# A gated cross-attention and expert kernel: GpSimd's scaling work and Newton steps dealt over the steps by a table, and VectorE's y tiles in two-tensor form

## The chip, the cores and the metric

One core of one Trainium2 chip runs the whole kernel. The metric is the device time of one execution in microseconds. The kernel before has a median of 321.2 us over 3 runs (321.14 to 321.3).

## The reference

Two residual blocks over x of shape (2, 1024, 256), all in float32:

```
x = x + tanh(g_xattn) * xattn(layernorm(x), ctx)     # 16 heads of 64, 64 context tokens
x = x + tanh(g_ffn)  * ffn(layernorm(x))             # 8 experts, top 2 of a sequence
layernorm(x) = (x - mean) / sqrt(var + 1e-5)
xattn: q = x Wq, k = ctx Wk / 8, v = ctx Wv, softmax(q k^T) v Wo + bo
ffn:   router on the mean over a sequence of layernorm(x); softmax, top 2 of 8
       sum over the two experts of  weight * (gelu(h w1 + b1) w2 + b2),  F = 1024
```

## The kernel before, in words

The 2048 tokens are 16 tiles of 128 tokens, t = 0 to 15; the first eight belong to sequence 0. After a setup of some 20 us, in which Wq and Wk are folded into one matrix and Wv and Wo into another, the attention runs as a software pipeline written out by hand: `run_steps` calls `step(s)` for s = -2 to 18 on every engine, each engine with its own order of work, and semaphores that count tiles tie them together. The order in the code is the order on the engine.

Every product is taken in three matmuls of rounded parts (high with high, high with low, low with high), so most tiles exist as `_hi` (written by ScalarE) and `_lo` (the rest, written by VectorE).

What tile t goes through, and at which step:

- x_scaled(t), only t >= 6, GpSimd, step t-2: `xs`, the raw x that was loaded already transposed, has the mean taken off and is multiplied with the reciprocal deviation. Both statistics lie in `spread`, where a DMA has copied them to all partitions. Tiles 0 to 5 are normalised untransposed (`xn`) and transposed by TensorE.
- x_high and x_low, ScalarE and VectorE, step t-1: `xT_hi`, `xT_lo`.
- scores(t), TensorE, step t: 12 matmuls of 512 columns.
- max(t) (L903), then the subtraction for 8 heads (L910), VectorE, step t; heads(t), ScalarE, step t: the exponentials of the other 8 heads (L636), right after max(t). The exponential of the first half follows at step t+1 (L625).
- sum and reciprocal (L873, L878), VectorE, step t+1; mul(t), GpSimd, step t+1: the product with the reciprocal in two halves (L504).
- transposes of tile t (L1238), TensorE, step t+2, then pT_high(t) (L648, ScalarE), pT_low(t) (L862, VectorE), then the value product, TensorE, which ends step t+2.
- residual(t) (L949) and its statistics (L954), VectorE, step t+3.

At steps 5 and 7 TensorE, ScalarE and VectorE also make the last four groups of the value matrix ("value groups": L1211, L600, L813); heads(s) stands behind them on ScalarE.

The second layernorm starts inside this pipeline. For each four tiles VectorE makes mean, variance and a first guess of the reciprocal root in eight small instructions on 4 columns (`norm` part 0, L762 to L770, called as `y_guess`, at steps 6, 10 and 14); GpSimd refines the guess by three Newton steps (`y_rstds`, L470 to L476, 13 small instructions that each wait for the one before) at the head of steps 7, 11 and 15, ahead of mul; VectorE then makes y tiles 0 to 7 (`y_tile`, L969) at the ends of steps 7 to 12, TensorE transposes them (L1326), and ScalarE and VectorE split them (L975). The same `norm` serves x: `x_norm(2)` for tiles 8 to 15 at VectorE's step 4, and its Newton steps at the end of GpSimd's step 4, whose result goes by DMA into `spread`. On GpSimd the order within a step is: y_rstds, `xn`, mul(s-1), x_scaled(s+2), Newton steps for x.

Behind the attention come the two experts of each sequence, in 64 pieces, TensorE with little idle time.

Of the kernel before, what the change touches and what calls it, by code (L numbers as in the profile page):

```python
# [5 lines left out]
def gated_cross_attention_moe_kernel(nc, x, xT, ctx_tokens, g_xattn, g_ffn, Wq, Wk, Wv, Wo, bo,  # L6
# [5 lines left out]
    ALU = mybir.AluOpType  # L12
# [4 lines left out]
    P = 128  # L17
# [18 lines left out]
    EPS = 1e-5  # L36
# [30 lines left out]

    stats2 = stats1
    mean1 = place("mean1", [P, NT])
    rstd1 = place("rstd1", [P, NT])  # L70
    mean2 = place("mean2", [P, NT])
    rstd2 = place("rstd2", [P, NT])
# [103 lines left out]
    with stack:  # L176
        ps = stack.enter_context(nc.psum_tensor("ps", [P, 8, BANK], f32))

        def sem(name):
            return stack.enter_context(nc.semaphore(name))  # L180
# [27 lines left out]
        rep_ready, logits_done, idx_ready, gap_ready, gap_done, sel_ready = (  # L208
            sem(n) for n in ("rep_ready", "logits_done", "idx_ready", "gap_ready", "gap_done", "sel_ready"))
        stat_out, stat_in, xT_raw, xT_ready = (sem(n) for n in ("stat_out", "stat_in", "xT_raw", "xT_ready"))  # L210
        y_rstd, x_rstd, xn_by_dve, w1_first = sem("y_rstd"), sem("x_rstd"), sem("xn_by_dve"), sem("w1_first")
        staged_w1 = [sem("staged_w1_0"), sem("staged_w1_1")]
        staged_half = [sem("staged_half_0"), sem("staged_half_1")]
# [132 lines left out]
        X_PARTS = [(0, TB // 2), (TB // 2, TB), (TB, NT)]  # L346

        X_BY_DVE = X_PARTS[1][0]
        SPREAD_PARTS = [(XT0, TB), (TB, NT)]
        x_stat = [nc.dram_tensor(f"x_stat_{i}", (2, P, t1 - t0), f32, kind="Internal").ap()  # L350
                  for i, (t0, t1) in enumerate(SPREAD_PARTS)]
# [10 lines left out]
        def active(t):  # L362
            return 0 <= t < NT
# [81 lines left out]
        @block.gpsimd  # L445
        def _(pool):
            nc.gpsimd.memset(ident[:, :], 0.0).then_inc(zeros_ready, 1)
            pool.wait_ge(zeros_ready, 1)
            nc.gpsimd.affine_select(out=ident[:, :], in_=ident[:, :], compare_op=ALU.not_equal, fill=1.0,
                                    base=0, pattern=[[-1, P]], channel_multiplier=1).then_inc(ident_ready, 1)  # L450
            nc.gpsimd.memset(ones_row[:, :], 1.0).then_inc(rows_ready, 1)
            for e in range(E):
                last = nc.gpsimd.memset(iota[:, e:e + 1], float(e))
            last.then_inc(rows_ready, 1)

            pn = [0]

            def link(ins):

                pn[0] += 1  # L460
                ins.then_inc(pool_step, 1)
                pool.wait_ge(pool_step, pn[0])

            def newton(t0, t1, rstd, var, guess):

                r, n = rstd[:, t0:t1], t1 - t0
                v, u = ve_p[:, 0:n], nu_p[:, 0:n]
                tt, ts = nc.gpsimd.tensor_tensor, nc.gpsimd.tensor_scalar
                pool.wait_ge(guess_ready, guess)
                link(ts(v, var[:, t0:t1], -0.5, None, ALU.mult))  # L470
                for _ in range(3):

                    link(tt(u, v, r, ALU.mult))
                    link(tt(u, u, r, ALU.mult))
                    link(ts(u, u, 1.5, None, ALU.add))
                    link(tt(r, u, r, ALU.mult))  # L476

            def y_rstds(i):

                newton(*Y_PARTS[i], rstd2, ve_y, len(X_PARTS) + i + 1)  # L480
                pool.sem_inc(y_rstd, 1)

            def step(s, par):
                if s in (7, 11, 15):
                    y_rstds((s - 7) // 4)
                t = s + LEAD
                if active(t) and t < XT0 and t != X_BY_DVE:

                    wait_pos(pool, xT_done, t - 1)
                    tile = xt[:, ds(t, 1), :].rearrange("p o d -> p (o d)")  # L490
                    nc.gpsimd.tensor_tensor(xn[:, par, :], tile, mean1[:, ds(t, 1)].broadcast_to([P, D]),
                                            ALU.subtract).then_inc(xc_ready, 1)
                    pool.wait_ge(xc_ready, t + (t < X_BY_DVE))
                    nc.gpsimd.tensor_tensor(xn[:, par, :], xn[:, par, :], rstd1[:, ds(t, 1)].broadcast_to([P, D]),
                                            ALU.mult).then_inc(xn_ready, 1)
                t = s - 1
                if active(t):
                    q = (par - 1) % 2

                    pool.wait_ge(recip_done, t + 1)  # L500
                    for half in range(2):
                        hs = slice(half * H // 2, (half + 1) * H // 2)
                        pr = sx[:, q, half * BANK:(half + 1) * BANK].rearrange("p (h m) -> p h m", m=M)
                        nc.gpsimd.tensor_tensor(pr, pr, rs[:, q, hs].unsqueeze(2).broadcast_to([P, H // 2, M]),  # L504
                                                ALU.mult).then_inc(mul_done, 1)
                if active(s + LEAD) and s + LEAD >= XT0:
                    x_scaled(s + LEAD)
                if s == 1:
                    newton(*X_PARTS[1], rstd1, ve_x, 2)
                    pool.sem_inc(x_rstd, 1)  # L510
                if s == 4:
                    newton(*X_PARTS[2], rstd1, ve_x, 3)
                    pool.sem_inc(x_rstd, 1)

            def x_scaled(t):

                i = next(i for i, (t0, t1) in enumerate(SPREAD_PARTS) if t < t1)
                mean, rstd = (spread[i][:, row, :, t - SPREAD_PARTS[i][0]].unsqueeze(1).broadcast_to([P, KD, P])
                              for row in range(2))
                pool.wait_ge(xT_raw, 32)  # L520
                pool.wait_ge(stat_in, 16 * (i + 1))
                nc.gpsimd.tensor_tensor(x_raw(t), x_raw(t), mean, ALU.subtract).then_inc(xc_ready, 1)  # L522
                pool.wait_ge(xc_ready, t)
                nc.gpsimd.tensor_tensor(x_raw(t), x_raw(t), rstd, ALU.mult).then_inc(xT_ready, 1)  # L524

            pool.wait_ge(guess_ready, 1)
            run_steps(step)


            pool.wait_ge(sel_ready, 1)  # L530
            for t in range(TB, NT):
                if t == Y_PARTS[3][0]:
                    pool.wait_ge(guess_ready, len(X_PARTS) + 4)
                pool.wait_ge(yT_done, t - 1)
                nc.gpsimd.tensor_tensor(yb[:, t % 2, :], xt[:, t, :], mean2[:, t:t + 1].broadcast_to([P, D]),
                                        ALU.subtract).then_inc(xc_ready, 1)
                pool.wait_ge(xc_ready, NT + t - TB)
                nc.gpsimd.tensor_tensor(yb[:, t % 2, :], yb[:, t % 2, :], rstd2[:, t:t + 1].broadcast_to([P, D]),
                                        ALU.mult).then_inc(y_ready, 1)
# [204 lines left out]
        def _(dve):  # L744
# [8 lines left out]
            def norm(t0, t1, mean, rstd, var, parts=range(4)):  # L753


                tiles, n = slice(t0, t1), t1 - t0
                me, ce, mo, co = (stats1[:, tiles, i] for i in (1, 2, 4, 5))
                m, r = mean[:, tiles], rstd[:, tiles]
                v, d, u = var[:, tiles], dm[:, 0:n], nu[:, 0:n]
                tt, ts, stt = nc.vector.tensor_tensor, nc.vector.tensor_scalar, nc.vector.scalar_tensor_tensor  # L760
                if 0 in parts:
                    tt(d, me, mo, ALU.subtract)  # L762
                    tt(m, me, mo, ALU.add)
                    link(tt(v, ce, co, ALU.add))
                    ts(m, m, 0.5, None, ALU.mult)
                    tt(d, d, d, ALU.mult)
                    link(ts(v, v, 1.0 / D, EPS, ALU.mult, ALU.add))
                    link(stt(v, d, 0.25, v, ALU.mult, ALU.add))

                    link(ts(r.bitcast(i32), v.bitcast(i32), -0.5, float(0x5F3759DF), ALU.mult, ALU.add))  # L770
                for part in (1, 2, 3):
                    if part in parts:

                        link(stt(u, v, -0.5, r, ALU.mult, ALU.mult))
                        link(tt(u, u, r, ALU.mult))
                        link(stt(r, u, 1.5, r, ALU.add, ALU.mult))
# [53 lines left out]
                                        ALU.subtract).then_inc(xlo_ready, 1)  # L830

            nc.vector.memset(warm_w[:, :], 0.0).then_inc(warm_ready, 1)
            dve.sem_inc(hlo_ready, FREE_GELS)
            group("ctxT", 0)
            x_stats(0, range(0, 2))
# [129 lines left out]
            def y_tile(t):  # L965

                dve.wait_ge(y_rstd, t // 4 + 1)
                wait_pos(dve, yT_done, t - 1)
                nc.vector.tensor_scalar(yb[:, t % 2, :], xt[:, t, :], mean2[:, t:t + 1], rstd2[:, t:t + 1],  # L969
                                        ALU.subtract, ALU.mult).then_inc(y_ready, 1)  # L970

            def y_low(t, bank, c0, until):

# [550 lines left out]
```

## Time and profile before

| | before |
|---|---|
| median of 3 runs | 321.2 us (321.14 to 321.3) |
| the profiled execution | 321.67 us, its span 319.7 us |
| granted TensorE clock | 0.999 of full speed |
| TensorE matmul busy | 313.2 us, 98% |
| VectorE busy | 236.5 us, 74% |
| ScalarE busy | 164.6 us, 52% |
| GpSimd busy | 84.5 us, 26% |

The profile is one execution with a start and a duration for every instruction. A row of a timeline gives the start in us from the span's start, the duration in us, the engine, the line, the operation and its tiles; "x2" means two merged instructions, and a bracket tells how long the engine had been idle and what released it. PE is TensorE, DVE is VectorE, ACT is ScalarE, POOL is GpSimd. Durations of neighbours can overlap a little, so the distance between two starts is the better measure of what an instruction costs its engine. The attention pipeline fills the time from about 23 to 140 us.

### The profile page before, as it was taken

Reading aid. Unit: us, or ns where it says so; the run is one execution under the profiler, and the core shown is the slowest. Engines: PE = TensorE matmul, PEld = TensorE weight load, DVE = VectorE, ACT = ScalarE, POOL = GpSimd, SP = SyncE. Lnnn points to the kernel's source line nnn. Section 1 sums busy time; section 2 is a strip of 40 time slices with the busy share of each in tenths; the row PEclk is TensorE's granted clock in tenths of the full one; section 3 lists DMA queues with packets and bytes.
Section 4 is the critical chain, followed back from the end, with each engine's and each line's share of the span. In section 5 each row is a group of like instructions: output and inputs, shape, how many; then the busy total and the mean of one; then the engine's idle time right before and its main releaser. Section 6 shows DMA issues by size and latency. Waiting matters only on the chain.

```text
span 319.7 us, 5709 instructions
## 1 busy us (share of the span) xinstructions
PE 313.2 (98%) x1861; PEld 269.9 (84%) x1861; DVE 236.5 (74%) x563; ACT 164.6 (52%) x577; POOL 84.5 (26%) x158
## 2 busy tenths in 40 slices
PE   8999999999999999999999999999999999999996
PEld 7878998878988999888788888888887899888896
DVE  1889999989989999999998475466767554442643
ACT  2648565686766768766366254444543442321320
POOL 1325547586476655425600000000000000000000
PEclk9999999999999999999999999999999999999999
DMA  7997300300000009500016250000020000000012
GB/s 261 386 330 9 35 3 1 133 1 3 0 0 3 0 2 331 195 3 0 2 8 255 79 187 0 0 0 0 24 99 11 2 0 0 2 0 0 2 66 67
DMA packets 21918, 19.99 MB, mean 63 GB/s; under 512 B 11708, under 2 KB 17540, under 8 KB 21508
## 3 DMA queue, kind: packets, MB, share of 16 engines
q1 hardware_dynamic: 21616, 19.14, 19.9%
q10 hardware_dynamic: 276, 0.52, 0.4%
q8 instruction: 14, 0.23, 0.3%
q14 instruction: 12, 0.10, 0.1%
HBM read 17.56 MB, written 2.11 MB: 62 GB/s over the span
## 4 chain that ended last, share of the span: by engine, by line
PE 71%; POOL 10%; DVE 7%; issue 7%; DMA 2%; ACT 2%; SPq 0%; POOLq 0%; DVEq 0%
PE ps L1153 22%; PE ps L1154 22%; PE ps L1155 22%; POOL sx L504 4%; DMA xt<-in_x_dram 2%; POOL xs L524 2%; PE ps L1238 2%; POOL xs L522 2%; ACT sx L636 1%; DVE mx L903 1%; PE ps L1173 1%; DVE pT_lo L862 1%; PE ps L1326 1%; DVE sm L873 1%; PE ps L1424 1%
## 5 line engine op out<-in xcount | busy, mean ns | idle before, releaser
L723 ACT ACTIVATE gel<-ps,b1sel 128x512 f32<-128x512 f32 x64 | 43.9, 690 | 95.5 <-PE ps L1155 95.4
L1112 DVE CAST h_hi<-gel 128x512 fp32r<-128x512 f32 x64 | 28.4, 444 | 58.8 <-ACT gel L723 58.5
L636 ACT ACTIVATE sx<-ps,mx 128x64 f32<-128x64 f32 x128 | 38.3, 325 | 26.2 <-DVE mx L903 26.1
L1153 PE MATMUL ps<-yT_hi,w_hi 128*128 128x512 f32 (+1 forms) x128 | 50.5, 395 | 0.0
L1154 PE MATMUL ps<-yT_lo,w_hi 128*128 128x512 f32 (+1 forms) x128 | 50.0, 390 | 0.0
L1155 PE MATMUL ps<-yT_hi,w_lo 128*128 128x512 f32 (+1 forms) x128 | 49.9, 390 | 0.0
L1114 DVE TENSOR_TENSOR h_lo<-gel,h_hi 128x512 fp32r<-128x512 f32 x64 | 44.9, 702 | 2.2
L504 POOL TENSOR_TENSOR sx<-sx,rs 128x512 f32<-128x512 f32 x32 | 33.5, 1066 | 41.5 <-DVE rs L878 40.8
L1153 PE MATMUL ps<-h_hi,w_hi 128*128 128x512 f32 x96 | 38.4, 400 | 0.0
L1155 PE MATMUL ps<-h_hi,w_lo 128*128 128x512 f32 x96 | 37.5, 390 | 0.0
L1154 PE MATMUL ps<-h_lo,w_hi 128*128 128x512 f32 x96 | 37.4, 390 | 0.0
L1153 PE MATMUL ps<-vw,pT_hi 128*128 128x256 f32 x128 | 36.6, 286 | 0.1
L1155 PE MATMUL ps<-vw,pT_lo 128*128 128x256 f32 x128 | 36.2, 283 | 0.0
L1154 PE MATMUL ps<-vw,pT_hi 128*128 128x256 f32 x128 | 36.2, 283 | 0.0
L1155 PEld LDWEIGHTS ps<-yT_hi,w_lo 128*128 128x128 f32 x128 | 24.0, 188 | 5.1
L1153 PEld LDWEIGHTS ps<-yT_hi,w_hi 128*128 128x128 f32 x128 | 24.1, 188 | 4.6
L1154 PEld LDWEIGHTS ps<-yT_lo,w_hi 128*128 128x128 f32 x128 | 24.1, 188 | 4.4
L636 ACT ACTIVATION_READ_ACCUMULATOR sx<-ps,mx 128x1 f32 x128 | 27.8, 217 | 0.0
L1153 PE MATMUL ps<-a_hi,xT_hi 128*128 128x512 f32 x64 | 26.5, 413 | 0.1
L1153 PEld LDWEIGHTS ps<-vw,pT_hi 128*128 128x128 f32 x128 | 24.4, 191 | 2.0 <-issue 1.4
L1155 PE MATMUL ps<-a_hi,xT_lo 128*128 128x512 f32 x64 | 25.1, 392 | 0.0
L1154 PE MATMUL ps<-a_lo,xT_hi 128*128 128x512 f32 x64 | 25.0, 390 | 0.0
(149 smaller groups left out, 670.3 us busy)
## 6 DMA issues: line engine op xcount, KB each, us to landing
stage_w<-in_L_ffn_w_dram SPq DMA_DIRECT2D x7, 1024.0 KB, 7.4
out_dram<-xt SPq DMA_DIRECT2D x6, 256.0 KB, 2.3
wqT<-in_L_xattn_Wq_dram SPq DMA_DIRECT2D x2, 512.0 KB, 7.2
wv_sb<-in_L_xattn_Wv_dram SPq DMA_DIRECT2D x2, 512.0 KB, 8.8
wo_sb<-in_L_xattn_Wo_dram SPq DMA_DIRECT2D x1, 1024.0 KB, 13.9
xt<-in_x_dram SPq DMA_DIRECT2D x1, 1024.0 KB, 10.6
xs<-in_xT_dram SPq DMA_DIRECT2D x1, 1024.0 KB, 11.1
spread<-x_stat SPq DMA_DIRECT2D x1, 1024.0 KB, 4.6
```

What stands on the lines that cost most here:

```text
L504: nc.gpsimd.tensor_tensor(pr, pr, rs[:, q, hs].unsqueeze(2).broadcast_to([P, H // 2, M]), ALU.mult).then_inc(mul_done, 1)
L522: nc.gpsimd.tensor_tensor(x_raw(t), x_raw(t), mean, ALU.subtract).then_inc(xc_ready, 1)
L524: nc.gpsimd.tensor_tensor(x_raw(t), x_raw(t), rstd, ALU.mult).then_inc(xT_ready, 1)
L636: last = nc.scalar.activation(sx[:, par, c0:c0 + M], ps[:, 2 * par + 1, c0 - BANK:c0 - BANK + M], ACT.Exp, bias=mx[:, par, h:h + 1], accum ...
L723: nc.scalar.activation(gel[:, f % 4, :], ps[:, h_bank, :], ACT.Gelu, bias=b1sel[:, b, slot, f:f + 1]).then_inc(gelu_done, 1)
L862: nc.vector.tensor_tensor(pT_lo[:, par, 4 * half:4 * half + 4, :], ps[:, 4 + half, :].rearrange("p (m i) -> p m i", m=4), as_f32(pT_hi[:, ...
L1112: nc.vector.tensor_copy(h_hi[:, f % 4, :], gel[:, f % 4, :]).then_inc(hhi_ready, 1)
L1114: nc.vector.tensor_tensor(h_lo[:, f % 4, :], gel[:, f % 4, :], as_f32(h_hi[:, f % 4, :]), ALU.subtract).then_inc(hlo_ready, 1)
L1153: mm(acc, hi_w, hi_x, start=start, stop=False)
L1154: mm(acc, hi_w, lo_x, start=False, stop=False)
L1155: return mm(acc, lo_w, hi_x, start=False, stop=stop)
L1238: last = nc.tensor.transpose(ps[:, 4 + half, m * P:(m + 1) * P], sx[:, par, c0:c0 + P], ident[:, :])
```

## The change

Four things. (1) x_scaled follows a table: tiles 6 and 7 at step 3 (before: 4 and 5), tile 12 at step 9 beside tile 11 (before: 10); the others stay. (2) GpSimd's Newton steps for y: the first at the head of step 6 (before: 7), the second in step 10 behind mul(9) (before: head of 11), the third stays at 15. (3) `norm` part 0 has seven instructions for eight, none of them but the guess in the one-tensor form: the mean is d * -0.5 + the first half's mean, and EPS comes from a column in SBUF, broadcast. It has five waits on itself for four. (4) `y_tile` is a scalar_tensor_tensor with the reciprocal deviation as a broadcast tensor, for a tensor_scalar with two per-partition scalars.

```diff
+    eps_col = place("eps_col", [P, 1])
+        SCALE_AT = {3: (6, 7), 6: (8,), 7: (9,), 8: (10,), 9: (11, 12), 11: (13,), 12: (14,), 13: (15,)}
@@ gpsimd
             def step(s, par):
-                if s in (7, 11, 15):
-                    y_rstds((s - 7) // 4)
+                if s in (6, 15):
+                    y_rstds((6, 10, 15).index(s))
...
-                if active(s + LEAD) and s + LEAD >= XT0:
-                    x_scaled(s + LEAD)
+                if s == 10:
+                    y_rstds((6, 10, 15).index(s))
+                for t in SCALE_AT.get(s, ()):
+                    x_scaled(t)
@@ vector, norm
                     tt(d, me, mo, ALU.subtract)
-                    tt(m, me, mo, ALU.add)
                     link(tt(v, ce, co, ALU.add))
-                    ts(m, m, 0.5, None, ALU.mult)
-                    tt(d, d, d, ALU.mult)
-                    link(ts(v, v, 1.0 / D, EPS, ALU.mult, ALU.add))
+                    stt(m, d, -0.5, me, ALU.mult, ALU.add)
+                    link(stt(v, v, 1.0 / D, eps_col[:, 0:1].broadcast_to([P, n]), ALU.mult, ALU.add))
+                    link(tt(d, d, d, ALU.mult))
                     link(stt(v, d, 0.25, v, ALU.mult, ALU.add))
@@ vector, at the start
+            nc.vector.memset(eps_col[:, :], EPS).then_inc(eps_ready, 1)
+            dve.wait_ge(eps_ready, 1)
@@ vector, y_tile
-                nc.vector.tensor_scalar(yb[:, t % 2, :], xt[:, t, :], mean2[:, t:t + 1], rstd2[:, t:t + 1],
-                                        ALU.subtract, ALU.mult).then_inc(y_ready, 1)
+                nc.vector.scalar_tensor_tensor(yb[:, t % 2, :], xt[:, t, :], mean2[:, t:t + 1],
+                                               rstd2[:, t:t + 1].broadcast_to([P, D]), ALU.subtract,
+                                               ALU.mult).then_inc(y_ready, 1)
```

## Rows read from the trace of the kernel before

**Rows 1.** The page, part 1: busy us (share of the span) xinstructions.
```profile
PE 313.2 (98%) x1861; PEld 269.9 (84%) x1861; DVE 236.5 (74%) x563; ACT 164.6 (52%) x577; POOL 84.5 (26%) x158
```

**Rows 2.** The page, part 4: the chain that ended last, by engine.
```profile
PE 71%; POOL 10%; DVE 7%; issue 7%; DMA 2%; ACT 2%; SPq 0%; POOLq 0%; DVEq 0%
```

**Rows 3.** Waits of PE: us in total, times, longest us.
```profile
PE ps L1238 <- POOL sx L504: 0.9, 3, 0.3
```

**Rows 4.** Timeline of DVE, steps 6 and 7: the loop.
```profile
61.35 1.21 DVE L903 TENSOR_REDUCE mx<-ps 128x16 f32<-128x1024 f32 x1
...
65.60 1.29 DVE L862 TENSOR_TENSOR pT_lo<-ps,pT_hi 128x512 fp32r<-128x512 f32 x2 [1.52 <-ACT pT_hi L648]
...
67.96 1.21 DVE L903 TENSOR_REDUCE mx<-ps 128x16 f32<-128x1024 f32 x1
```

**Rows 5.** Timeline of ACT, steps 5 to 7.
```profile
49.41 1.12 ACT L648 ACTIVATE pT_hi<-ps 128x512 fp32r<-128x512 f32 x2
...
64.92 1.13 ACT L648 ACTIVATE pT_hi<-ps 128x512 fp32r<-128x512 f32 x2
...
67.85 1.27 ACT L600 ACTIVATE vw<-ps,tg 128x512 fp32r<-128x512 f32 x2 [0.98 <-PE ps L1211]
```

**Rows 6.** Timeline of DVE, step 4's x_norm(2) and pT_low behind it.
```profile
47.77 0.72 DVE L763 TENSOR_TENSOR mean<-stats 128x8 f32<-128x8 f32 x1
...
48.61 0.70 DVE L765 TENSOR_SCALAR mean<-mean 128x8 f32<-128x8 f32 x1
...
50.83 1.27 DVE L862 TENSOR_TENSOR pT_lo<-ps,pT_hi 128x512 fp32r<-128x512 f32 x2
```

**Rows 7.** Timeline of POOL, steps 4 to 9: scaling, Newton steps, mul.
```profile
47.72 0.74 POOL L522 TENSOR_TENSOR xs<-xs,spread 128x256 f32<-128x256 f32 x1
...
50.02 0.24 POOL L470 TENSOR_SCALAR ve_p<-ve_x 128x8 f32<-128x8 f32 x1 [0.73 <-DVEq L794]
...
54.10 2.04 POOL L504 TENSOR_TENSOR sx<-sx,rs 128x512 f32<-128x512 f32 x2 [0.18 <-POOL rstd L476]
...
61.23 2.09 POOL L504 TENSOR_TENSOR sx<-sx,rs 128x512 f32<-128x512 f32 x2 [3.58 <-DVE rs L878]
63.29 0.85 POOL L522 TENSOR_TENSOR xs<-xs,spread 128x256 f32<-128x256 f32 x1
...
65.10 0.23 POOL L470 TENSOR_SCALAR ve_p<-ve_y 128x4 f32<-128x4 f32 x1
...
82.03 2.10 POOL L504 TENSOR_TENSOR sx<-sx,rs 128x512 f32<-128x512 f32 x2 [3.00 <-DVE rs L878]
```

**Rows 8.** Timeline of DVE, step 6's y_guess and pT_low behind it.
```profile
57.77 0.17 DVE L762 TENSOR_TENSOR dm<-stats 128x4 f32<-128x4 f32 x1
...
57.93 0.16 DVE L764 TENSOR_TENSOR ve_y<-stats 128x4 f32<-128x4 f32 x1
58.12 0.17 DVE L765 TENSOR_SCALAR mean<-mean 128x4 f32<-128x4 f32 x1
...
58.99 1.29 DVE L862 TENSOR_TENSOR pT_lo<-ps,pT_hi 128x512 fp32r<-128x512 f32 x2
```

**Rows 9.** Timeline of PE: the first matmul of scores(7), step 7.
```profile
63.80 0.48 PE L1153 MATMUL ps<-a_hi,xT_hi 128*128 128x512 f32 x1
```

**Rows 10.** Timeline of DVE, y_tile(0) and pT_low(6), steps 7 and 8.
```profile
71.13 1.02 DVE L969 TENSOR_SCALAR yb<-xt,mean,rstd 128x256 f32<-128x256 f32 x1
...
72.86 1.27 DVE L862 TENSOR_TENSOR pT_lo<-ps,pT_hi 128x512 fp32r<-128x512 f32 x2
```

**Rows 11.** Timeline of DVE, step 10's y_guess and pT_low behind it.
```profile
86.00 0.17 DVE L762 TENSOR_TENSOR dm<-stats 128x4 f32<-128x4 f32 x1
...
87.21 1.29 DVE L862 TENSOR_TENSOR pT_lo<-ps,pT_hi 128x512 fp32r<-128x512 f32 x2
```

**Rows 12.** Groups of DVE by form: busy us, mean ns of one, idle before.
```profile
L894 DVE TENSOR_TENSOR xT_lo<-xs,xT_hi 128x256 fp32r<-128x256 f32 x10 | 3.6, 361 | 0.0
...
L883 DVE TENSOR_SCALAR xn<-xt,mean,rstd 128x256 f32<-128x256 f32 x1 | 0.3, 327 | 0.0
```

More of the change, by code:

```diff
@@ L210, in gated_cross_attention_moe_kernel @@
         stat_out, stat_in, xT_raw, xT_ready = (sem(n) for n in ("stat_out", "stat_in", "xT_raw", "xT_ready"))
+        eps_ready = sem("eps_ready")
         y_rstd, x_rstd, xn_by_dve, w1_first = sem("y_rstd"), sem("x_rstd"), sem("xn_by_dve"), sem("w1_first")
```

## The prediction

> **What bounds the kernel now.** I read the page's busy line first: TensorE is busy for 98% of the span, so anything that helps must take away idle or late TensorE work, and the whole reserve is some 6 us of 319.7 [rows 1]. The chain of waits then gives GpSimd 10% of the chain's length, far more than its share of necessary work would suggest, and VectorE 7% [rows 2]. The waits of TensorE put only 0.9 us on GpSimd's mul [rows 3]. That is the first hint: direct stalls are small, and what counts is how a late instruction travels round the pipeline. So I went to the timelines of the four engines and followed one step.
>
> The timelines show a loop between VectorE and ScalarE. max(6) starts at 61.35, pT_high(5) at 64.92 once heads(6) is done, pT_low(5) at 65.60 (0.68 behind pT_high), and max(7) at 67.96: 6.61 us for a step [rows 4, 5]. From pT_low to the next max are 2.36; from the start of max to pT_high 3.57, of which max with its handover takes 1.24 and heads 2.33. Hence, whatever makes pT_low late makes every later tile late, unless TensorE is later still. pT_low can be late for two reasons: VectorE is not free yet, or heads on ScalarE started late. I work out both, place by place, as the lateness of this loop against before.
>
> How the engines disturb each other is in two rows. GpSimd's first scaling instruction of tile 6 runs from 47.72 to 48.46 [rows 7]. VectorE's L763, an addition of 8 columns with both inputs in SBUF, starts at 47.77 and takes 0.72, to 48.49, and L765 takes 0.70 the same way behind the second scaling instruction [rows 6]; without GpSimd beside them such instructions take 0.16 to 0.17 [rows 8]. L763 is a two-tensor instruction, L765 a one-tensor one: both forms are held to the end of GpSimd's instruction. A two-tensor form doesn't escape.
>
> **The change, part by part.**
>
> *x_scaled(6) and (7) at step 3.* They leave step 4 and take with them the two holds on x_norm(2): (0.72 - 0.16) + (0.70 - 0.17) = 1.1 us. The new form of x_norm costs 0.05 more (below). pT_low(3), which stands behind, can't start before pT_high(3) at 49.41 plus 0.68 = 50.09; it started at 50.83. The loop gains 0.74, the rest of the 1.1 is VectorE waiting. At step 3 the pair (1.6 us) fits into GpSimd's idle time before mul(3), since GpSimd idles 3.6 us before a mul [rows 7]. Value: -0.74; bounds 0 (should `spread` land late and the pair slip back) and -0.74.
>
> *Newton steps at the head of step 6.* They can start only when y_guess(0) ends, which in the new kernel is 58.99 - 0.74 + 0.05 = 58.3 [rows 8]. From the first Newton instruction to the mul behind it took 54.10 - 50.02 = 4.08; some of that was waiting for others, and I take 3.9. So mul(5) starts at 62.2. It started at 61.23 and, with the loop 0.74 ahead, could start at 60.5 [rows 7]. mul(5) is thus 1.7 late against what it could be, and 1.0 late against before. TensorE's second half of transposes needs it, and scores(7) moves from 63.80 to 64.8 [rows 9]. Behind scores(7) come the value groups of step 7; ScalarE's part of these waited for TensorE at 67.85 and takes 1.27 [rows 5]; it moves to 68.8 and ends at 70.0. heads(7) stands behind it, and before it started with the end of max(7), 67.96 + 1.24 = 69.2. So heads(7) is 0.8 late.
>
> *Newton steps gone from step 7.* They began at 65.10 and by the same 4.08 made mul(6) start at 69.2 [rows 7], though reciprocal(6) is done before max(7) at 67.96 [rows 4]. y_tile(0) then met the scaling of tile 9 head on, and was held for 1.02 us instead of 0.33 [rows 10, 12]; pT_low(6) started at 72.86, when ScalarE would have allowed 67.96 + 3.57 + 0.68 = 72.2. In the new order mul(6) starts at 67.2, scaling ends at 67.2 + 2.06 + 1.81 = 71.1, y_tile(0) comes at 70.9 and is held little. But ScalarE is late now: heads(7) at 70.0 + 2.33 + 0.68 gives pT_low(6) at 73.0. Against 72.86 that is +0.1. The 0.74 is used up: this place costs 0.84. Bounds: 0.1 (if mul(5) is only 0.3 late in effect) and 1.3 (all of 58.3 + 4.08 passed on, and the hold too).
>
> *x_scaled(12) at step 9, against y_guess(1) at step 10.* mul(8) starts at 82.03 + 0.1; it takes 2.06, each scaling pair 1.81 (63.29 to 65.10) [rows 7]. Tile 11 is at work from 84.2 to 86.0 and tile 12 from 86.0 to 87.8. y_guess(1) starts at 86.00 + 0.1 [rows 11]: exactly beside tile 12's two instructions, where GpSimd was idle before. By the rows of x_norm(2) its small instructions are held twice for most of a scaling instruction, and the chain gets on by one or two of its seven before GpSimd is through at 87.8; the remaining five take about 0.9. y_guess(1) ends at 88.7 instead of 87.21, and pT_low(8) directly behind it starts when it ends, before as after. Value: +1.4 on top of the +0.1; bounds 0.05 (no hold) and 1.8 (no progress in the gap).
>
> *Newton steps behind mul(9).* From 3.9 us in front of mul(10) they go into GpSimd's idle time behind mul(9), with x_scaled(12) cleared out of their way. This frees TensorE of a wait in step 12 (one of the three in rows 3), but the loop was ahead of mul(10) only on TensorE's side; I count nothing, bounds -0.4 and 0.
>
> *The small instructions of norm.* The starts are 0.08 apart without a wait between them and 0.19 with one (57.77, 57.93, 58.12) [rows 8]. Eight with four waits took 1.22 (57.77 to 58.99); seven with five take 0.05 more. Twice this stands in pT_low's way, but it is contained above.
> The Trainium skill (VectorE: DVE Perf Modes, Rules for kernel authors) says to minimise the number of operations, not the semaphores; by that seven for eight would save about 0.15, and the sum would be 0.3 us less. The rows bear it out only for instructions that wait anyway.
>
> *y_tile in two-tensor form.* The nearest rows are 0.36 for a two-tensor 128x256 in SBUF and 0.33 for the old form [rows 12]; a second per-partition operand less, a full stream more. Most tiles are held by a scaling instruction as before. I take 0.1 for each of eight and hide it in the 0.68 between pT_high and pT_low, except in steps 11 and 12 with two tiles each, where VectorE is already the later one; there VectorE later also waits for less (the routing step), so I count 0. Bounds -0.3 and +0.5. The new EPS column costs one small memset in the setup, where VectorE waits for loads: nothing.
>
> **The sum**, against the profiled execution of 321.67 us (span 319.7): -0.74 + 0.84 + 1.4 + 0 = +1.5, so 323.2 for a profiled execution. The median before is 0.47 lower, 321.2; hence 322.7. TensorE has so little idle time after the attention that nothing there takes up a later start.
>
> **Rivals.**
>
> *A: VectorE's small instructions slip past GpSimd.* If y_guess(1) is not held, the 1.4 goes: -0.74 + 0.84 + 0.05 = +0.15, 321.3. For it: L764, the instruction between the two held ones, wasn't held (L763 ends at 48.49 and L765 starts at 48.61 [rows 6]). Against it: the two that didn't, and that the chain needs every one of its instructions.
>
> *B, the other side: faster.* One mechanism: Newton in step 6 delays nobody. mul(5) is late, but pT_high(5) can't start before heads(6) ends at 64.2, and if the value groups of step 7 have slack, the place costs nothing and keeps the unheld y_tile(0) (-0.65) beside the -0.74. It decides if mul(5)'s second half is through by 63.3 as before, that is, if Newton's 13 instructions take under 3.0 us. With y_guess(1) half held (+0.7) that gives -0.7, 320.5; with it unheld -1.35, 319.9. Against it: the 4.08 us in the rows.
>
> *C: the late mul(5) also pushes x_scaled(8).* Its scaling would end at 62.2 + 2.06 + 1.81 = 66.1, and ScalarE wants it once pT_high(5) and the exponential are done, some 1.5 us behind the 64.3 at which pT_high(5) begins (an estimate from the 1.13 of rows 5). If this slips by 0.5, step 8 starts later: +0.7 more, 323.4 to 323.8.
>
> **Chances.** Forecast (322.0 to 323.3): 0.50; C: 0.10; A: 0.22; B: 0.18. A measurement of this kernel can tell 0.2% (0.64 us) from no change: slower 0.60 (forecast and C), the same 0.22 (A), faster 0.18 (B). The range of 320.4 to 323.8 takes in A and C and the upper part of B. The forecast's own range is 322.0 to 323.4.
>
> **What would show it.** Right: L763's successor in x_norm(2) at its plain 0.16 and pT_low(3) at about 50.1; mul(5) at about 62.2, directly behind L476; the value groups on ScalarE at 68.8; two instructions of y_guess(1) near 0.7 us each, and max(10) 1.5 us later than the 89.9 at which 87.21 + 2.36 + about 0.33 for y_low (an estimate from the 0.36 of rows 12) puts it. Wrong: y_guess(1) at 1.3 us in all beside a busy GpSimd (A), or mul(5) before 61.3 (B). Should the loop be 1.5 late at step 10 and the time unchanged, then TensorE, not the loop, sets the end.

## The result, and the profile after

The changed kernel took 325.3 us (median of 6 runs, 323.24 to 325.39), the kernel before 321.3 us on the same chip (321.14 to 321.57, 6 runs). The ratio is 1.0106, with a 95% interval of 1.0088 to 1.0123: slower by 4.0 us, where I had forecast 1.5, and above the top of my range, 323.8. The profiled execution took 325.37 us, its span 323.6.

The six times form two groups: 325.25 to 325.39 (four, mean granted clock 0.995) and 323.24 and 323.62 (two, clock 1.0, called calm executions from here on).

The page of the changed kernel, busy line, granted clock in 40 slices, and chain by engine (answers to [rows 1, 2]; before the change every one of the 40 digits was a 9):

```profile
PE 315.1 (97%) x1861; PEld 270.6 (84%) x1861; DVE 237.0 (73%) x557; ACT 164.6 (51%) x577; POOL 85.0 (26%) x158
PEclk9999999979999999999999999999999999999999
PE 71%; DVE 15%; ACT 6%; issue 4%; DMA 2%; POOL 1%; SPq 0%; DVEq 0%; ACTq 0%; POOLq 0%
```

The one 7 lies at 65 to 73 us. The waits of TensorE in the changed kernel (us in total, times, longest), which answer to [rows 3]:

```profile
PE ps L1245 <- POOL sx L507: 1.9, 3, 1.3
PE ps L1160 <- DVE pT_lo L868: 0.7, 1, 0.7
```

The total on mul has gone from 0.9 to 1.9, and one wait alone is 1.3. GpSimd in the changed kernel, steps 6 to 10 (answers to [rows 7]): the first Newton instruction, mul(5), then the scalings of tiles 11 and 12.

```profile
58.45 0.23 POOL L473 TENSOR_SCALAR ve_p<-ve_y 128x4 f32<-128x4 f32 x1 [3.18 <-DVEq L969]
...
62.59 2.04 POOL L507 TENSOR_TENSOR sx<-sx,rs 128x512 f32<-128x512 f32 x2 [0.18 <-POOL rstd L479]
...
87.23 0.92 POOL L529 TENSOR_TENSOR xs<-xs,spread 128x256 f32<-128x256 f32 x1
88.12 0.92 POOL L527 TENSOR_TENSOR xs<-xs,spread 128x256 f32<-128x256 f32 x1
89.12 0.90 POOL L529 TENSOR_TENSOR xs<-xs,spread 128x256 f32<-128x256 f32 x1
```

TensorE in the changed kernel, around scores(7) (answers to [rows 9]), then three rows of the same place in the kernel before, and then the stretch of the changed kernel by windows (length; busy us of PE, PEld, DVE, ACT, POOL; granted clock; DMA):

```profile
63.68 0.66 PE L1245 MATMUL ps<-ident,sx 128*128 128x128 f32 x4 [1.30 <-POOL sx L507]
64.68 0.66 PE L1245 MATMUL ps<-ident,sx 128*128 128x128 f32 x4 [0.34 <-POOL sx L507]
65.09 0.48 PE L1160 MATMUL ps<-a_hi,xT_hi 128*128 128x512 f32 x1
...
66.59 0.63 PE L1161 MATMUL ps<-a_lo,xT_hi 128*128 128x512 f32 x1
67.02 0.63 PE L1162 MATMUL ps<-a_hi,xT_lo 128*128 128x512 f32 x1
...
69.61 1.09 PE L1218 MATMUL ps<-wo_sb,vT_sb 64*64 64x256 f32 x16
```

```profile
64.34 0.40 PE L1155 MATMUL ps<-a_hi,xT_lo 128*128 128x512 f32 x1
64.57 0.39 PE L1153 MATMUL ps<-a_hi,xT_hi 128*128 128x512 f32 x1
...
66.71 1.09 PE L1211 MATMUL ps<-wo_sb,vT_sb 64*64 64x256 f32 x16
```

```profile
62.00:64.00 2.00, 0.70 (x7) 0.50 (x6) 1.47 (x4) 1.94 (x13) 1.74 (x4) 1.00 0.00 0
64.00:66.00 2.00, 1.66 (x11) 1.27 (x9) 0.69 (x1) 1.65 (x7) 1.92 (x3) 0.88 0.00 0
66.00:68.00 2.00, 2.00 (x6) 1.51 (x6) 1.81 (x4) 0.85 (x2) 0.75 (x2) 0.50 0.04 8
68.00:70.00 2.00, 2.00 (x14) 1.33 (x16) 0.28 (x1) 0.00 (x0) 2.00 (x3) 0.77 0.00 0
```

This is the heart of the case. TensorE stands still for 1.30 and 0.34 us while it waits for mul(5), with the clock at 1.00; then the granted clock falls to 0.50, that is from 2.4 to 1.2 GHz. Two matmuls of scores(7) start 0.43 apart (66.59 and 67.02), where the kernel before had 0.23 (64.34 and 64.57). From the first scores matmul to the value group behind them are 4.5 us (65.09 to 69.61); before they were 2.9 (63.80 to 66.71), so scores(7) itself became 1.6 us longer. TensorE is "2.00 busy" in both slow windows: the busy share shows nothing, only the clock's column does. The Trainium skill (TensorE: Matmul & The Clock Gate, Part 1: The HAM clock gate) says that this gate passes either half of the clock or all of it, and nothing between. The 0.50 agrees, and the 0.88 and 0.77 are then windows in which it changed.

VectorE in the changed kernel (answers to [rows 4, 6, 8, 10, 11]):

```profile
47.91 0.17 DVE L768 TENSOR_TENSOR ve_x<-stats 128x8 f32<-128x8 f32 x1
50.22 1.29 DVE L868 TENSOR_TENSOR pT_lo<-ps,pT_hi 128x512 fp32r<-128x512 f32 x2 [0.21 <-ACT pT_hi L653]
...
60.81 1.21 DVE L909 TENSOR_REDUCE mx<-ps 128x16 f32<-128x1024 f32 x1
69.72 1.23 DVE L909 TENSOR_REDUCE mx<-ps 128x16 f32<-128x1024 f32 x1 [1.87 <-PE ps L1162]
72.91 0.47 DVE L975 SCALAR_TENSOR_TENSOR yb<-xt,mean,rstd 128x256 f32<-128x256 f32 x1
77.65 1.23 DVE L909 TENSOR_REDUCE mx<-ps 128x16 f32<-128x1024 f32 x1
...
88.27 0.80 DVE L767 TENSOR_TENSOR dm<-stats 128x4 f32<-128x4 f32 x1
88.99 0.16 DVE L768 TENSOR_TENSOR ve_y<-stats 128x4 f32<-128x4 f32 x1
89.18 0.86 DVE L769 SCALAR_TENSOR_TENSOR mean<-dm,stats 128x4 f32<-128x4 f32 x1
90.86 1.29 DVE L868 TENSOR_TENSOR pT_lo<-ps,pT_hi 128x512 fp32r<-128x512 f32 x2
102.34 1.93 DVE L975 SCALAR_TENSOR_TENSOR yb<-xt,mean,rstd 128x256 f32<-128x256 f32 x2
```

The starts of max are the milestones by which I compare kernels. Starts in us, read from the timelines; a kernel's setup shifts them by up to 0.35, which the last column takes out (change of the distance from max(3) to max(15), against before):

| kernel | max(3) | max(5) | max(6) | max(7) | max(8) | max(10) | max(13) | max(15) | change |
|---|---|---|---|---|---|---|---|---|---|
| before | 39.22 | 53.17 | 61.35 | 67.96 | 75.54 | 89.90 | 110.87 | 124.26 | 0 |
| changed | 39.36 | 52.58 | 60.81 | 69.72 | 77.65 | 93.55 | 114.84 | 128.23 | +3.83 |
| e1 table | 39.43 | 52.65 | 60.83 | 67.44 | 75.02 | 90.71 | 111.62 | 125.01 | +0.54 |
| e2 Newton | 39.19 | 53.13 | 61.31 | 68.64 | 76.55 | 90.96 | 114.98 | 128.50 | +4.27 |
| e3 y_tile | 38.89 | 52.85 | 61.04 | 67.65 | 75.36 | 89.87 | 111.31 | 124.69 | +0.76 |
| e4 norm | 39.13 | 53.15 | 61.38 | 67.98 | 75.55 | 89.97 | 110.92 | 124.31 | +0.14 |
| e5 | 39.40 | 52.61 | 60.85 | 67.46 | 75.16 | 91.06 | 112.39 | 125.75 | +1.31 |
| e6 | 38.88 | 52.11 | 60.35 | 67.82 | 75.73 | 91.67 | 113.02 | 126.41 | +2.49 |
| e7 | 39.32 | 52.55 | 60.79 | 68.09 | 76.00 | 90.57 | 111.89 | 125.26 | +0.90 |
| e8 | 39.29 | 52.50 | 60.70 | 67.30 | 74.88 | 89.24 | 110.19 | 123.56 | -0.77 |
| e9 | 39.24 | 52.45 | 60.63 | 67.24 | 74.81 | 89.17 | 110.07 | 123.44 | -0.84 |
| e10 | 39.23 | 52.45 | 60.69 | 67.30 | 75.01 | 89.56 | 110.87 | 124.25 | -0.02 |
| e11 | 39.22 | 52.45 | 60.67 | 68.00 | 75.92 | 91.82 | 112.72 | 126.11 | +1.85 |
| e12 | 39.23 | 53.19 | 61.37 | 70.28 | 78.25 | 92.64 | 113.59 | 126.97 | +2.70 |

The changed kernel, read along its row: 0.7 ahead at max(5) (with the setup taken out), then 2.65 lost between max(6) and max(8), 1.54 between max(8) and max(10), and 0.32 between max(10) and max(13).

### The profile page after: what moved, and what is told of

It is laid out like the page before. It is cut to its first block, busy times and chain, and to the rows that moved or that the text cites. A ratio compares the mean times of both kernels' runs of the same rounds, so it can differ in the third digit from the quotient of the medians.

```text
span 323.6 us, 5703 instructions
## 1 busy us (share of the span) xinstructions
PE 315.1 (97%) x1861; PEld 270.6 (84%) x1861; DVE 237.0 (73%) x557; ACT 164.6 (51%) x577; POOL 85.0 (26%) x158
## 4 chain that ended last, share of the span: by engine, by line
PE 71%; DVE 15%; ACT 6%; issue 4%; DMA 2%; POOL 1%; SPq 0%; DVEq 0%; ACTq 0%; POOLq 0%
PE ps L1160 22%; PE ps L1162 21%; PE ps L1161 21%; ACT sx L641 4%; DVE mx L909 3%; DVE pT_lo L868 3%; DVE sm L879 2%; DMA xt<-in_x_dram 2%; PE ps L1245 2%; PE ps L1180 1%; DVE xT_lo L900 1%; ACT pT_hi L653 1%; PE ps L1333 1%; DVE vw L817 1%; DVE yb L975 1%
## 5 line engine op out<-in xcount | busy, mean ns | idle before, releaser
L1162 PE MATMUL ps<-a_hi,xT_lo 128*128 128x512 f32 x64 | 25.8, 403 | 0.0
```

What stands on the lines that cost most here:

```text
L1162: return mm(acc, lo_w, hi_x, start=False, stop=stop)
```

## The experiments

Four kernels first, each with one part of the change in the kernel before (which had 321.73 us in these runs).

**e1, the table alone.**

```diff
+SCALE_AT = {3: (6, 7), 6: (8,), 7: (9,), 8: (10,), 9: (11, 12), 11: (13,), 12: (14,), 13: (15,)}
-if active(s + LEAD) and s + LEAD >= XT0:
-    x_scaled(s + LEAD)
+for t in SCALE_AT.get(s, ()):
+    x_scaled(t)
```

> The kernel before with the scaling table alone. Theory (place and hold): tiles 6 and 7 at step 3 free x_norm(2), -0.7 us; tile 12 at step 9 lies beside y_guess(1) at step 10 and holds two of its small instructions, in their old forms too, +1.5. Together +0.4 to +0.8: 321.7 to 322.1, pT_low(8) about 0.8 us later than its 87.21. No fall of TensorE's clock. Rival (the new instruction forms are what costs): the table alone gains, 320.5.

Measured: 322.26 us (322.06 to 322.39), ratio 1.0017 (1.0008 to 1.0026). It is 0.7 ahead at max(6) and loses 1.3 by max(10). VectorE's y_guess(1) in e1, with the eight old instructions:

```profile
85.48 0.87 DVE L763 TENSOR_TENSOR dm<-stats 128x4 f32<-128x4 f32 x1
...
86.53 0.80 DVE L766 TENSOR_SCALAR mean<-mean 128x4 f32<-128x4 f32 x1
```

Tile 12 at step 9 thus costs most of its price (1.33 between max(8) and max(10)) without the new forms, and a one-tensor instruction is held as a two-tensor one is. With the new forms of norm the same place costs 1.54; where the other 0.2 comes from no run separates.

**e2, the Newton steps alone**, at the head of step 6 and in step 10 behind mul(9).

```diff
-if s in (7, 11, 15):
-    y_rstds((s - 7) // 4)
+if s in (6, 15):
+    y_rstds((6, 10, 15).index(s))
...
+if s == 10:
+    y_rstds((6, 10, 15).index(s))
```

> The kernel before with the Newton steps moved alone. Theory: mul(5) starts at about 63 instead of 61.23, TensorE idles over a us before it and its granted clock falls for scores(7); and in step 10 the scaling of tile 12, which now follows the Newton steps, makes mul(10) late. 323.6 if the clock holds, 325.2 if it falls, perhaps both among its runs. Rival (the clock has another cause): 323.6 at most with a flat clock.

Measured: 326.02 us (324.89 to 326.52), ratio 1.0133 (1.0115 to 1.0151): worse than the whole change, and above both of the times expected; the one run with the clock at 1.0 had 324.89, where 323.6 was expected. In its profile max(8) is 1.0 late with the clock at 1.00. The large loss lies at max(10) to max(13). Here tile 12 is still scaled in step 10, now behind the Newton steps, so mul(10) comes late; waits and windows of e2:

```profile
PE ps L1240 <- POOL sx L504: 2.5, 4, 1.3
PE ps L1328 <- DVE yb L971: 1.3, 1, 1.3
```

```profile
100.00:103.00 3.00, 1.14 (x9) 0.76 (x8) 2.96 (x6) 1.75 (x13) 2.31 (x3) 1.00 0.00 0
103.00:106.00 3.00, 3.00 (x10) 2.37 (x10) 2.39 (x5) 3.00 (x14) 0.00 (x0) 0.60 0.03 8
```

The same picture in another place: TensorE mostly idle (1.14 busy of 3.00), and then a clock of 0.60.

**e3, y_tile alone** in the two-tensor form.

```diff
-nc.vector.tensor_scalar(yb[:, t % 2, :], xt[:, t, :], mean2[:, t:t + 1], rstd2[:, t:t + 1],
-                        ALU.subtract, ALU.mult)
+nc.vector.scalar_tensor_tensor(yb[:, t % 2, :], xt[:, t, :], mean2[:, t:t + 1],
+                               rstd2[:, t:t + 1].broadcast_to([P, D]), ALU.subtract, ALU.mult)
```

> The kernel before with y_tile in two-tensor form alone. Theory: each held tile ends 0.13 us later (256 elements at one per cycle instead of two), felt only at steps 11 and 12: +0.2 to +0.4, 321.5 to 321.7. Rival (a two-tensor form is not held by GpSimd): y_tile at 0.4 us each and 320.8.

Measured: 322.48 us (322.05 to 322.8), ratio 1.0026 (1.0016 to 1.0037). I had priced this at nothing, and expected 0.2 to 0.4 for this run; it costs 0.75.

**e4, norm alone** (seven instructions for eight, the EPS column; the diff is that of part 3 of the change).

> The kernel before with the new form of the small statistics instructions (and the EPS column) alone. Theory: one more wait and one instruction less, +0.05 each time, and +0.1 from the EPS memset in the setup: 321.4 to 321.6. Rival (they escape the hold at x_norm(2)): pT_low(3) at 50.1 and 320.6.

Measured: 321.63 us (321.32 to 322.85; the highest stands alone, 1.15 above the next, with the clock at 1.0, and no run explains it), ratio 1.0000 (0.9991 to 1.0009). x_norm(2) in e4, with tile 6 still scaled beside it:

```profile
47.67 0.72 DVE L765 TENSOR_TENSOR ve_x<-stats 128x8 f32<-128x8 f32 x1
...
48.52 0.72 DVE L767 SCALAR_TENSOR_TENSOR ve_x<-ve_x,eps_col 128x8 f32<-128x8 f32 x1
```

The holds stay, 0.72 each, near the 0.72 and 0.70 of [rows 6]. The milestones show 0.05 to 0.07 more in each of the three places with a norm, 0.14 in all, as forecast; the time doesn't show it. At y_guess(1) the seven instructions took 1.25 us (86.02 to 87.27 in e4), the eight 1.21 (86.00 to 87.21): one instruction less, with one wait more, saved nothing.

The next four (the kernel before: 321.54 us) ask what makes the changed kernel lose.

**e5, the changed kernel with the first Newton steps back at step 7.**

```diff
-if s in (6, 15):
-    y_rstds((6, 10, 15).index(s))
+if s in (7, 15):
+    y_rstds((7, 10, 15).index(s))
```

> The changed kernel with its first Newton steps back at the head of step 7. Theory: mul(5) starts about 60.7, TensorE doesn't idle before it, its clock stays at full speed in every run, and the loop is level with before at step 8; what is left is the hold in step 10 and 0.3 at steps 11 to 13: 322.2 to 322.5, with no second group of times. Rival (the clock falls for another reason): 324 or more.

Measured: 322.86 us (322.48 to 322.93), ratio 1.0035 (1.0022 to 1.0047), clock 0.999 or 1.0 in all five runs; 0.4 above the range expected, which had 0.3 for steps 11 to 13, where the milestones have 0.4. This one move accounts for 2.3 of the 4.0 us (1.0106 - 1.0035 = 0.0071 of 321.5).

**e6, the changed kernel with TensorE's gap filled**: ten matmuls of zeros, which the trace shows as twenty instructions, at the head of TensorE's step 7, nothing else moved.

```diff
 def step(s, par):
     t = s - 2
+    if s == 7:
+        warm_up(10)
```

> The changed kernel with ten idle-filling matmuls of zeros (128x128) on TensorE at the head of step 7, where it waits for mul(5). Theory (the clock fell because TensorE stood idle): mul(5) is as late as in the changed kernel, but scores(7) runs at full clock: 323.4 in all runs, like the changed kernel's two quick runs. Rival (the lateness is all in the waits, the clock is a bystander): 325.3 as before the filling.

Measured: 323.76 us (323.44 to 323.89), ratio 1.0066 (1.0053 to 1.0079), clock 0.999 or 1.0 in all five runs. TensorE and GpSimd in e6:

```profile
61.78 2.39 PE L1156 MATMUL ps<-warm_w 128*128 128x128 f32 x20
```

```profile
62.13 2.04 POOL L507 TENSOR_TENSOR sx<-sx,rs 128x512 f32<-128x512 f32 x2 [0.18 <-POOL rstd L479]
```

mul(5) is as late as in the changed kernel (23.25 behind max(3), there 23.23), but in no run does the clock fall. With work that computes nothing the kernel is 0.4% faster than the changed kernel's median, in which most executions fell, and no faster than its calm executions: 323.43 / 321.31 = 1.0066. The filling is also a little too long: scores(7) starts 4.45 behind max(6) (64.80 in e6's timeline), in the changed kernel, e7 and e11 4.28 or 4.29, and 0.15 of e6's time is this.

**e7, the changed kernel with tile 11 at step 8**, so that tile 12 is through earlier.

```diff
-SCALE_AT = {..., 8: (10,), 9: (11, 12), ...}
+SCALE_AT = {..., 8: (10, 11), 9: (12,), ...}
```

> The changed kernel with tile 11 scaled at step 8 beside tile 10 and tile 12 alone at step 9, so that GpSimd is through before y_guess(1). Theory (the hold in step 10 costs 1.5 us): y_guess(1) takes 1.3 us in all and the time falls by 1.4 to 1.6 against the changed kernel: 323.8 where the clock falls, 321.9 where it doesn't. Rival (the hold is taken up by slack on TensorE): a fall under 0.5.

Measured: 322.17 us, ratio 1.0028 (1.0014 to 1.0042); ten runs between 321.90 and 322.46 with the clock at 0.999 or 1.0, two at 323.98 and 324.05 with 0.995; expected were 321.9 and 323.8. y_guess(1) is not held, and max(10) comes 1.5 earlier than in e6 (by the distances from max(3)). TensorE and the window behind it in e7's profile, and VectorE:

```profile
63.66 0.66 PE L1245 MATMUL ps<-ident,sx 128*128 128x128 f32 x4 [1.30 <-POOL sx L507]
```

```profile
66.00:68.00 2.00, 2.00 (x13) 1.38 (x11) 1.80 (x4) 0.88 (x2) 0.79 (x2) 1.00 0.03 8
```

```profile
86.62 0.17 DVE L767 TENSOR_TENSOR dm<-stats 128x4 f32<-128x4 f32 x1
86.89 0.17 DVE L769 SCALAR_TENSOR_TENSOR mean<-dm,stats 128x4 f32<-128x4 f32 x1
```

TensorE idles exactly as in the changed kernel, 1.30, and in this execution the clock stays at 1.00. So the idle time doesn't bring the fall each time; it opens the door to it.

**e8, only tiles 6 and 7 moved**, in the kernel before.

```diff
+SCALE_AT = {3: (6, 7), 6: (8,), 7: (9,), 8: (10,), 9: (11,), 10: (12,), 11: (13,), 12: (14,), 13: (15,)}
...
```

> The kernel before with tiles 6 and 7 scaled at step 3 and nothing else. Theory: x_norm(2) is not held and pT_low(3) starts at about 50.1; the loop is 0.7 us ahead to the end: 320.6. Rival (what is gained there is lost again at the held y_tile(0) or on TensorE): 321.2.

Measured: 320.90 us (320.67 to 321.08), ratio 0.9978 (0.9969 to 0.9986): the one part that gains, 0.6 to 0.7 us, near the 320.6 expected. VectorE in e8:

```profile
47.75 0.16 DVE L763 TENSOR_TENSOR dm<-stats 128x8 f32<-128x8 f32 x1
...
50.13 1.29 DVE L863 TENSOR_TENSOR pT_lo<-ps,pT_hi 128x512 fp32r<-128x512 f32 x2 [0.26 <-ACT pT_hi L649]
```

The last four (the kernel before: 321.70 us) test the account so far.

**e9, the gain without the losses**: the kernel before with a table and Newton steps in the places that cost nothing, old forms throughout.

```diff
+SCALE_AT = {3: (6, 7), 6: (8,), 7: (9,), 8: (10, 11), 9: (12,), 11: (13,), 12: (14,), 13: (15,)}
-if s in (7, 11, 15):
+if s in (7, 15):
...
+if s == 10:
+    y_rstds((7, 10, 15).index(s))
...
```

> The kernel before with three parts of the idea placed where the runs so far say they cost nothing: tiles 6 and 7 scaled at step 3, tiles 10 and 11 at step 8, 12 at step 9, the first Newton steps left at the head of step 7, the second behind mul(9); the norm and y_tile keep the old forms. My theory (each of the changed kernel's losses has its own place: tile 12 beside y_guess(1), Newton ahead of mul(5), the two-tensor y_tile): x_norm(2) unheld, -0.7 to -0.8 from step 5 on; y_guess(1) unheld, max(10) no later than -0.7 against before; nothing falls in the granted clock; 320.5 to 320.8 us where the kernel before is 321.5, ratio 0.997 to 0.998. Rival (Newton behind mul(9) frees TensorE's wait in step 12, which I had bounded at -0.4): 320.2 or less. Rival (moving tile 11 to step 8 holds VectorE there as tile 12 did at step 10): no better than 321.3.

Measured: 320.91 us (320.6 to 321.05), ratio 0.9976 (0.9967 to 0.9985): faster than both kernels, by what e8 alone gives. y_guess(1) runs at 0.17 an instruction, and TensorE's wait on mul, 0.9 in [rows 3], is gone from its list; yet from max(10) to max(13) it takes 20.90 where before took 20.97. Removing those waits is worth 0.07 at most, not the 0.4 of the rival: they were hidden. In e1 the stretch takes 20.91 as well, and there the Newton steps stand at step 11 as before; so the move of the Newton steps behind mul(9) shows no gain of its own.

**e10, the changed kernel with both repairs** (e5 and e7 together).

> The changed kernel with both repairs at once: first Newton steps back at the head of step 7, tile 11 scaled at step 8 beside tile 10; its two-tensor y_tile and its norm stay. Theory: only the gain of step 3 (-0.74), the price of the two-tensor y_tile (+0.76 when alone) and of the norm (0 to 0.1) are left, so the time is that of the kernel before within 0.2 us, 321.4 to 321.7 where before is 321.5, and 0.7 to 0.9 above the old-form version of the same order. Rival (the two repairs share one gain, as both stand before the same step 10): 322.1 or more, as either alone.

Measured: 321.44 us (320.9 to 321.59), ratio 0.9992 (0.9983 to 1.0001): no difference from before, as the theory had it. Against e9, which differs only in the forms, it is 0.53 slower by the medians and 0.82 by the milestones of the two profiles; 0.7 to 0.9 had been expected.

**e11, the changed kernel with y_tile in the old form.**

> The changed kernel with y_tile alone put back to the one-tensor form. Theory (in the changed kernel only the tiles of steps 12 and 13 have VectorE as the later engine, so the form costs 0.33 there, by its trace): 0.3 to 0.4 less than the changed kernel, 324.9 in executions where TensorE's clock falls in step 7 and 323.2 where it doesn't. Rival (the form costs its full 0.76 here too): 324.5 and 322.7.

Measured: 323.09 us (322.86 to 323.29), ratio 1.0043 (1.0030 to 1.0056), all five runs calm. The changed kernel's calm executions have 1.0066, so by the times the form costs 0.0023 of 321.5, 0.7 us, as the rival has it; but that rests on two calm executions, 0.4 apart, and on ratios to two measurements of the kernel before, 321.31 and 321.70. By the milestones it costs 0.4 to 0.45, near the theory: from max(10) to max(13) the changed kernel, e5, e6 and e7 take 21.29 to 21.35 and e11 20.90, and nowhere else is there a difference in the changed kernel's order (step 7, from max(7) to max(8), is 7.91 in e6 and e7, 7.92 in e11). Which of the two is nearer stays open. The two y tiles of step 12 in e11, to set beside the 1.93 at 102.34 in the changed kernel:

```profile
100.61 1.72 DVE L975 TENSOR_SCALAR yb<-xt,mean,rstd 128x256 f32<-128x256 f32 x2
```

With the first Newton steps at step 7 the form costs more by the milestones: e10 and e3 also take 0.13 or 0.14 more from max(7) to max(8) than e9 and the kernel before. With them at step 6 VectorE waits for ScalarE's pT_high(6) there, 0.22 us in e11, and that part is hidden.

**e12, the first Newton steps alone at the head of step 6**, in the kernel before.

```diff
-if s in (7, 11, 15):
-    y_rstds((s - 7) // 4)
+if s in (6, 11, 15):
+    y_rstds((6, 11, 15).index(s))
```

> The kernel before with the first Newton steps alone at the head of step 6, the others left at 11 and 15. Theory: mul(5) is about 1.7 late (62.9 to 63.0), TensorE idles over 1 us before the second transposes of step 7; where the granted clock stays at full speed, max(8) and max(10) come 1.0 to 1.1 late (my forecast's term was 0.84), 322.5 us; where it falls behind that idle time, another 1.6 on top, 324.1. The times then fall in two groups 1.6 apart. Rival (the fall needs the 0.74 gain ahead of it, or the late tiles later on, and has nothing to do with the late mul(5)): all times in one group at 322.5.

Measured: four runs at 322.44 to 322.87 with the clock at 0.999 to 1.0, and two at 324.24 and 324.42 with 0.994: two groups, 1.5 apart, as expected. The median of all is 322.86, the ratio 1.0043 (1.0028 to 1.0059). Its profile is one of the two; TensorE, windows and VectorE in e12:

```profile
64.24 0.66 PE L1238 MATMUL ps<-ident,sx 128*128 128x128 f32 x4 [1.30 <-POOL sx L504]
```

```profile
66.00:68.00 2.00, 2.00 (x6) 1.52 (x6) 1.70 (x4) 1.42 (x3) 0.89 (x2) 0.50 0.03 8
```

```profile
70.28 1.23 DVE L903 TENSOR_REDUCE mx<-ps 128x16 f32<-128x1024 f32 x1 [1.86 <-PE ps L1155]
```

The same gap, the same 0.50, the same wait of max(7) (1.87 in the changed kernel). The rival, that the fall needs the other parts of the change, is out.

**Gap and fall counted over all runs.** The kernels with Newton at the head of step 6 and the gap unfilled (changed, e2, e7, e11, e12) fell in 4 of 6, 4 of 5, 2 of 12, 0 of 5 and 2 of 6 runs: 12 of 34. In e2's profile the fall stands behind its second gap and not behind this one (clock 1.00 from 64 to 70 us); without e2 it is 8 of 29. All others (the kernel before, e1, e3 to e6, e8 to e10) fell in none of over 140. (The place of the fall is known for the profiled executions alone; for the others the mean clock of 0.994 or 0.995 and the time tell it.) That a gap is needed is thus shown, by the fall right behind one in three profiles (changed, e12, e2) and by these counts. Shorter waits of TensorE didn't bring it: the kernels that never fell have single ones of up to 0.7 us in the attention pipeline (pT_low(8) in e5, 0.73). That filling the gap protects isn't shown: e6 had 0 of 5, but e11 had 0 of 5 unfilled. What decides in which execution the clock falls stays open.

## Why the prediction was wrong

The direction was right; the size was outside the range. Term by term, as differences from before in the distances between milestones:

| term | forecast | measured |
|---|---|---|
| x_scaled(6,7) at step 3 | -0.74 | -0.72 (e11 at max(5)), -0.77 (e8) |
| Newton at step 6 and gone from 7 | +0.84 | +1.06 (e11, max(6) to max(8)), +1.05 (e2) |
| the same, when the clock falls | none | +1.6 more (changed and e12, max(6) to max(8)) |
| tile 12 at step 9 | +1.4 | +1.54 (e11 and changed, max(8) to max(10)); +1.33 with the old norm (e1) |
| Newton behind mul(9) | 0 | -0.07 at most |
| norm | in the above | +0.14 alone (e4) |
| y_tile | 0 | +0.76 alone (e3); +0.4 in the changed kernel (max(10) to max(13), against e11) |

Without the fall these come to -0.72 + 1.06 + 1.54 - 0.07 + 0.4 = +2.2 by the milestones, and the calm executions were 323.43 - 321.31 = 2.1 slower by the time of the whole run. With it the sum is 3.8; the milestones have 3.83 and the whole run 4.0.

- **The step that failed** is "Newton steps at the head of step 6". Its times came out: mul(5) at 62.59 where I had 62.2, directly behind the last Newton instruction. But I took the wait on TensorE as lateness alone, "mul(5) is thus 1.7 late ... scores(7) moves from 63.80 to 64.8". scores(7) did start at 65.09, 0.3 later than that. But its duration I took over unchanged: 2.9 us to the value group. In the profiled execution it ran largely at 1.2 GHz and took 4.5; the other three with the same mean clock have the same time. By the times of whole runs the fall costs 1.9 in the changed kernel (325.36 against 323.43) and in e7, 1.5 in e12. Nothing in the prediction gives the late mul(5) a price of this kind. The calm executions, 323.4, lie inside the range, but 0.7 above the forecast of 322.7.
- **The mis-sized term** is y_tile. I had the bounds right in kind (+0.5 above) but took 0, as VectorE there "later also waits for less". One that meets nobody takes 0.47 in the changed kernel (72.91) and 0.42 in e11's timeline (93.67); two in a row beside a scaling take 1.93 against 1.72. From max(10) on VectorE is the later one, and nothing hides it. In e3 this adds up to 0.76, more than my bound; in the changed kernel the form cost 0.4 by the milestones and 0.7 by the times.
- **y_guess(1)** went as forecast, or nearly: two instructions held, 0.80 and 0.86, where I said "near 0.7 us each"; and pT_low(8) stood right behind the chain, at 90.86. Rival A (the small ones slip past) is out: they pass only where GpSimd is idle, as in e7 and e9, or between two of its instructions, as L768 at 88.99. The Trainium skill (SBUF — State Buffer, Who interferes with whom) has it that the one which starts second is blocked for the whole of the first's instruction; the 0.80 at 88.27 ends with GpSimd's 88.12 + 0.92, so the trace agrees.
- **The value groups** on ScalarE stood at 69.04 in e11, where I had 68.8, and pT_low(6) at 73.20, where I had 73.0; this 0.2 is the whole miss of that term (+1.06 for +0.84).
- **Rival B** (Newton at step 6 delays nobody) is out by e12: it needed the Newton steps in under 3.0 us, and they took 4.14 in the changed kernel (58.45 to 62.59); **C** (x_scaled(8) pushed) named the time of the calm executions, but for a reason that the timelines don't bear out: in the changed kernel tile 8 is scaled by 65.53 + 0.87 = 66.40, and x_high(8) on ScalarE starts at 66.44 directly behind the exponential, which starts at 65.87 and takes 0.62. That its number fits the calm executions is luck.

## What to carry to other kernels

A wait on the busiest engine has two prices: the time it lasts, and what the engine's clock does behind it. Read the granted clock by windows behind the longer idle times of TensorE (here 1.3 us brought a fall in some executions, and 0.7 in none), and keep a chance for the lower level in the range, as it comes in some executions only. Before a loaded engine's work is moved, ask who starts beside it: of four moves here the one that took a GpSimd instruction away from small VectorE instructions gained 0.7, and the one that put one beside them lost 1.3 to 1.5.

## What the runs showed of the hardware

- After 1.30 + 0.34 us of idle time in an otherwise full pipeline TensorE's granted clock fell from 2.4 to 1.2 GHz in some executions only: 4 of 6 of the changed kernel, 2 of 6 of e12, 2 of 12 of e7, none of 5 of e11. In e2, with a second, longer gap (1.86 of 3.00 us), the mean clock was lower in 4 of 5, and in its profile the fall came behind that second gap. TensorE was busy for 2.00 of 2.00 us while it was slow.
- With twenty matmul instructions on zeros in the gap it fell in none of five runs (e6); as it fell in none of five of e11 either, that the filling did this isn't shown.
- No execution of a kernel whose single idle times of TensorE in the attention pipeline stay at or below about 0.7 us had the lower mean clock (none of over 140).
- Small VectorE instructions of 4 or 8 columns, one-tensor and two-tensor alike, took 0.7 to 0.9 us where they started while a GpSimd scaling ran (0.80 and 0.86 in the changed kernel, 0.87 and 0.80 in e1, 0.72 twice in e4), and 0.15 to 0.17 otherwise.
